# A six-layer local-attention kernel: weight splits and rotary products made once in the global stage, kept in DRAM, and fetched at the layer borders

## What is computed

```python
for i in range(DEPTH):                                   # DEPTH = 6
    x = attn_layer(shift_tokens(x), Wqkv[i], q_scale[i], k_scale[i], Wo[i]) + x
    x = ffn_layer(shift_tokens(x), ln_g[i], ln_b[i], W1[i], b1[i], W2[i], b2[i]) + x
# attn_layer: 16 heads of 64, q and k normalised, scaled by q_scale/k_scale, turned by rotary
# tables that depend on the position, attention inside windows of 32 tokens and the one before
```

## Time and profile before

| what | us |
|---|---|
| median of 3 runs | 3338.78 (3337.55 to 3340.59) |
| the profiled execution | 3341.1 |
| its span, first to last instruction | 3339.3 |
| PE, DVE, ACT, POOL busy | 3236.8, 2646.8, 2627.2, 2300.2 |
| mean granted TensorE clock | 0.989 of full |

### The profile page before, as it was taken

How to read it: one execution, slowest core, us unless ns; L and a number is a source line. 1 busy time by engine, 2 the same in 40 slices (tenths; PEclk the granted TensorE clock), 3 DMA queues, 4 the chain that set the end, 5 groups by cost and what they waited for, 6 DMA issues and landing times. The chain is left out here.

```text
span 3339.3 us, 125688 instructions
## 1 busy us (share of the span) xinstructions
PE 3236.8 (97%) x50357; PEld 2579.0 (77%) x50357; DVE 2646.8 (79%) x6351; ACT 2627.2 (79%) x5453; POOL 2300.2 (69%) x1519
## 2 busy tenths in 40 slices
PE   7979999999999999999999999999999999999997
PEld 5758878877877877887877787877788777778785
DVE  4658878878888877887887888878788787888884
ACT  3448888888888888888888888888888888888883
POOL 2028777777777776777777777777777777777771
PEclk9989999999999999999999999999999999999998
DMA  2001111211211211211221111121111121111111
GB/s 88 3 4 50 44 41 48 69 39 41 56 44 40 73 42 40 55 45 40 56 58 42 49 49 42 40 72 43 47 48 45 40 73 40 49 43 49 42 40 48
DMA packets 98194, 156.51 MB, mean 47 GB/s; under 512 B 18128, under 2 KB 39632, under 8 KB 96720
## 3 DMA queue, kind: packets, MB, share of 16 engines
q1 hardware_dynamic: 93440, 132.73, 14.8%
q10 hardware_dynamic: 4176, 15.74, 1.4%
HBM read 20.48 MB, written 2.10 MB: 7 GB/s over the span
## 5 line engine op out<-in xcount | busy, mean ns | idle before, releaser
L316 POOL TENSOR_TENSOR qks<-work 128x1024 f32<-128x1024 f32 x384 | 910.5, 2371 | 113.3 <-issue 105.7
L324 POOL TENSOR_TENSOR qkr<-qks,rnorm 128x1024 f32<-128x1024 f32 x384 | 731.4, 1905 | 307.6 <-issue 221.5
L493 ACT ACTIVATE sq<-psum 128x512 f32<-128x512 f32 x768 | 461.4, 601 | 234.8 <-PE psum L737 233.2
L332 POOL TENSOR_TENSOR probn<-prob,psumr 128x512 f32<-128x512 f32 x384 | 400.5, 1043 | 303.3 <-DVE psumr L1104 303.3
L737 PE MATMUL psum<-whi,xhi 128*128 128x512 f32 x1152 | 552.5, 480 | 24.6 <-POOL xlo L341 18.6
L1056 DVE TENSOR_REDUCE ssq<-sq 128x8 f32<-128x512 f32 x768 | 519.9, 677 | 8.1 <-ACT sq L493 7.9
L1080 DVE TENSOR_TENSOR work<-psum,rot 128x512 f32<-128x512 f32 x768 | 508.8, 662 | 8.3 <-POOL qks L316 7.5
L757 PEld LDWEIGHTS psum<-kT,qbd 128*64 128x64 f32 x12288 | 392.3, 139 | 154.9 <-issue 100.4
L1098 DVE TENSOR_REDUCE psumr<-prob 128x8 f32<-128x512 f32 x384 | 261.9, 682 | 287.5 <-ACT prob L547 283.1
L737 PE MATMUL psum<-whi,xlo 128*128 128x512 f32 x1152 | 459.6, 399 | 0.0
L757 PE MATMUL psum<-kT,qbd 128*64 128x64 f32 x12288 | 445.6, 226 | 13.1 <-ACT kT L529 13.1
(11 more groups left out here) (131 smaller groups left out, 6385.7 us busy)
## 6 DMA issues: line engine op xcount, KB each, us to landing
vsh<-vtok SPq DMA_DIRECT2D x384, 192.0 KB, 2.5
vsh<-vtok SPq DMA_DIRECT2D x384, 64.0 KB, 2.7
xsh<-xs_in SPq DMA_DIRECT2D x192, 64.0 KB, 2.1
ff_x<-x_mid SPq DMA_DIRECT2D x96, 128.0 KB, 2.4
wqkv<-Wqkv_dram ACTq DMA_DIRECT2D x5, 1536.0 KB, 7.8
wo_next<-Wo_dram ACTq DMA_DIRECT2D x5, 512.0 KB, 10.6
xtok<-x_dram SPq DMA_DIRECT2D x4, 512.0 KB, 11.0
out_dram<-qkr SPq DMA_DIRECT2D x8, 256.0 KB, 2.6
```

The lines of the kernel that those rows point to most:

```text
L316: pool.tensor_tensor(qks[:, :, :], rcos, rsin, ALU.add).then_inc(s["add_ready"], 1)
L324: pool.tensor_tensor(qkr[:, n % 2, :, :], qks[:, :, :], rnorm[:, :].unsqueeze(2).to_broadcast([P, 2 * OCT, DH]), ALU.mult).then_inc(s["qkr ...
L332: pool.tensor_tensor(probn[:, :, :], prob[:, n % 2, :, :], psumr[:, n % 2, 1, :].unsqueeze(2).to_broadcast([P, OCT, KEYS]), ALU.mult).then ...
L493: act.activation(sq[:, w * OCT:(w + 1) * OCT, :], bank[w].rearrange("p (h n) -> p h n", n=DH), ACT.Square).then_inc(s[("sqq_ready", "sqk_r ...
```

## The change

The splits of all six layers and the products of rotary table and scales of all six layers are made by POOL in the global stage, and those of layers 1 to 5 are written to DRAM by SP. POOL first makes six rotary products of 128x2048 (`rotary_gains(layer)`), then 18 pieces of weights (`weights_split(j)`, three a layer, each a copy of 128x1024 for the high part and a subtraction of 128x1024 for the low part). `global_inverse(1)` to `global_inverse(5)` stand between the groups of three pieces; numbers 6 and 7 stand behind all of it and behind three memsets. SP fetches the raw pieces of 512 KB (two in flight), and stores five rotary products and 15 pieces of 1 MB each; two staging buffers each, so that POOL waits for the store before last.

In the loop SP fetches a section (512 KB, high and low part) into its place as soon as PE has made the last projection of the old layer with it: the sections of q and k of the even units at step -2 of the border, those of the odd units at step -1, those of v at steps 1 and 2. It fetches the rotary products of a half sequence (512 KB) at steps -6 and 2, and `wo` straight into its place at step 6, all in its one queue behind `values_shifted` of the same step and ahead of `x_half` of the next. ACT's and POOL's split instructions, the copy of `wo`, POOL's `rotary_gains` and the two DMAs of ACT's queue are gone from the loop. Several buffers of the loop (`kT`, `qbd`, `vtok` among them) lie over the staging buffers; their memsets come behind the last store, and PE's first projection waits for them (`overlays_set`). The weights lie in DRAM in the order of the sections, which the host arranges.

```diff
@@ constants and buffers
+SECTION_AT = {wo: k for k, wo in enumerate(SECTIONS)}
+PIECES = len(SECTIONS) // 2
...
-        rot = sb("rot", [P, TPI, 2, 2, DH])
-        wqkv = sb("wqkv", [P, 3, INNER])
-        whi = sb("whi", [P, 3, INNER], F32R)
-        wlo = sb("wlo", [P, 3, INNER], F32R)
+        rot = sb("rot", [P, TPB, 2, 2, DH])
+        wparts = sb("wparts", [P, len(SECTIONS), 2, 512], F32R)
-        wo_next = sb("wo_next", [P, INNER // P, D])
...
+        with ExitStack() as early:
+            rot_raw = early.enter_context(nc.sbuf_tensor("rot_raw", [P, TPB, 2 * 2 * DH], F32))
+            qk_gain = early.enter_context(nc.sbuf_tensor("qk_gain", [P, DEPTH, 2 * 2 * DH], F32))
+            wraw = early.enter_context(nc.sbuf_tensor("wraw", [P, 2, 2, 512], F32))
+            rstage = shared("rstage", [P, 2, TPB, 2 * 2 * DH])
+            wstage = early.enter_context(nc.sbuf_tensor("wstage", [P, 2, 2, 2, 512], F32R))
...
+        wsplit = nc.dram_tensor("wsplit", (DEPTH - 1, len(SECTIONS), P, 2 * 512), F32, kind="Internal").ap()
+        rsplit = nc.dram_tensor("rsplit", (DEPTH - 1, P, TPB * 2 * 2 * DH), F32, kind="Internal").ap()
@@ sync
-            sp.dma_start(wqkv[:, :, :].rearrange("p k n -> p (k n)"), Wqkv[0]).then_inc(s["wqkv_in"], 16)
+            def raw_fetched(j):
+                layer, k = j // PIECES, j % PIECES
+                sp.dma_start(wraw[:, j % 2, :, :].rearrange("p s n -> p (s n)"), Wqkv[layer][:, k * 1024:(k + 1) * 1024]).then_inc(wraw_in[j % 2], 16)
+
+            def split_stored(j):
+                layer, k = j // PIECES, j % PIECES
+                sp.dma_start(wsplit[layer - 1, 2 * k:2 * k + 2].rearrange("s p n -> p s n"),
+                             wstage[:, j % 2, :, :, :].bitcast(F32).rearrange("p s h n -> p s (h n)")).then_inc(w_stored[j % 2], 16)
+
+            raw_fetched(0)
+            raw_fetched(1)
...
+            for layer in range(1, DEPTH):
+                sp.wait_ge(s["rot_made"], layer + 1)
+                sp.dma_start(rsplit[layer - 1], rstage[:, layer % 2, :, :].rearrange("p t n -> p (t n)")).then_inc(r_stored[layer % 2], 16)
+            for j in range(DEPTH * PIECES):
+                sp.wait_ge(s["w_lo"], j + 1)
+                if j + 2 < DEPTH * PIECES:
+                    raw_fetched(j + 2)
+                if j >= PIECES:
+                    split_stored(j)
+
+            def section_renewed(layer, k):
+                if layer is None:
+                    return
+                w, oc = SECTIONS[k]
+                if layer == 1 and k == 0:
+                    for half in range(2):
+                        sp.wait_ge(w_stored[half], 16 * ((DEPTH * PIECES - PIECES + half) // 2))
+                sp.wait_ge(s[("projq_ready", "projk_ready", "vp_ready")[w]], layer * UNITS - 1 + oc)
+                sp.dma_start(wparts[:, k, :, :].bitcast(F32).rearrange("p h n -> p (h n)"), wsplit[layer - 1, k]).then_inc(wparts_in[k], 16)
+
+            def rotation_renewed(layer, half):
...
+                sp.wait_ge(s["rotk_ready"], layer * UNITS - (1 - half) * UNROLL)
+                sp.dma_start(rot[:, half * TPI:(half + 1) * TPI, :, :, :].rearrange("p t k n d -> p (t k n d)"),
+                             rsplit[layer - 1][:, half * TPI * 4 * DH:(half + 1) * TPI * 4 * DH]).then_inc(rot_in[half], 16)
+
+            def output_renewed(layer):
...
+                sp.wait_ge(s["wo_ready"], layer * TILES)
+                sp.dma_start(wo[:, :, :].rearrange("p k n -> p (k n)"), Wo[layer]).then_inc(s["wo_in"], 16)
@@ sync, the loop over steps
                 x_half(step)
                 ffn_fetched(block_at(step, 1))
                 values_shifted(step - 4)
+                rotation_renewed(renewed_at(step, -6), 0)
+                section_renewed(renewed_at(step, -2), SECTION_AT[0, 0])
+                section_renewed(renewed_at(step, -2), SECTION_AT[1, 0])
+                section_renewed(renewed_at(step, -1), SECTION_AT[0, 1])
+                section_renewed(renewed_at(step, -1), SECTION_AT[1, 1])
+                section_renewed(renewed_at(step, 1), SECTION_AT[2, 0])
+                section_renewed(renewed_at(step, 2), SECTION_AT[2, 1])
+                rotation_renewed(renewed_at(step, 2), 1)
+                output_renewed(renewed_at(step, 6))
@@ gpsimd
+            def rotary_gains(layer):
+                if layer >= 3:
+                    pool.wait_ge(r_stored[layer % 2], 16 * ((layer - 1) // 2))
+                dst = rstage[:, layer % 2, :, :] if layer else rot[:, :, :, :, :].rearrange("p t k n d -> p t (k n d)")
+                pool.tensor_tensor(dst, rot_raw[:, :, :], qk_gain[:, layer:layer + 1, :].to_broadcast([P, TPB, 4 * DH]),
+                                   ALU.mult).then_inc(s["rot_made"], 1)
+
+            def weights_split(j):
+                layer, k, slot = j // PIECES, j % PIECES, j % 2
+                pool.wait_ge(wraw_in[slot], 16 * (j // 2 + 1))
+                if j in (PIECES, PIECES + 1):
+                    pool.wait_ge(r_stored[1], 16 * 3)
+                    pool.wait_ge(r_stored[0], 16 * 2)
+                elif layer:
+                    pool.wait_ge(w_stored[slot], 16 * ((j - PIECES) // 2))
+                parts = wstage[:, slot, :, :, :] if layer else wparts[:, 2 * k:2 * k + 2, :, :]
+                pool.tensor_copy(parts[:, :, 0, :], wraw[:, slot, :, :]).then_inc(s["w_hi"], 1)
+                pool.wait_ge(s["w_hi"], j + 1)
+                pool.tensor_tensor(parts[:, :, 1, :], wraw[:, slot, :, :], parts[:, :, 0, :].bitcast(F32), ALU.subtract).then_inc(s["w_lo"], 1)
 
             global_inverse(0)
-            for k in range(len(SECTIONS)):
-                weights_low(0, k)
-            for n in range(1, 2 * B):
+            pool.wait_ge(s["gain_in"], 16 * 2)
+            for layer in range(DEPTH):
+                rotary_gains(layer)
+            for j in range(DEPTH * PIECES):
+                if j and j % PIECES == 0:
+                    global_inverse(j // PIECES)
+                weights_split(j)
+            for half in range(2):
+                pool.wait_ge(w_stored[half], 16 * ((DEPTH * PIECES - PIECES + half) // 2))
+            pool.memset(kT[:, :, 0:WIN], 0.0)
+            pool.memset(qbd[:, :, :, :, :], 0.0)
+            pool.memset(vtok[:, 1, :, :], 0.0).then_inc(s["overlays_set"], 1)
+            for n in range(DEPTH, 2 * B):
                 global_inverse(n)
...
-                low_renewed(renewed_at(step, -1), 0, 1)
-                low_renewed(renewed_at(step, 0), 2, 3)
-                low_renewed(renewed_at(step, 2), 4)
-                low_renewed(renewed_at(step, 3), 5)
-                rotary_gains(step)
                 x_low(step)
@@ scalar
-                    if i in (1, 2, 3) and b == 0:
-                        weights_high(0, 2 * i - 2)
-                        weights_high(0, 2 * i - 1)
...
-                weights_fetched(renewed_at(step, -8))
-                output_renewed(renewed_at(step, 6))
-                high_renewed(renewed_at(step, -1), 0, 1)
-                high_renewed(renewed_at(step, 0), 2, 3)
-                high_renewed(renewed_at(step, 2), 4)
-                high_renewed(renewed_at(step, 3), 5)
@@ tensor, project
-                if n % UNITS < UPT:
-                    pe.wait_ge(s["w_lo"], n // UNITS * len(SECTIONS) + ((0, 1), (2, 3), (4, 5))[oc if w < 2 else 2][w if w < 2 else oc] + 1)
+                if n % UNITS < UPT and n >= UNITS:
+                    pe.wait_ge(wparts_in[SECTION_AT[w, oc]], n // UNITS * 16)
@@ vector, rotation
-                need(dve, "rot_made", n // UPT + 1)
+                if w == 0 and n == 0:
+                    dve.wait_ge(s["rot_made"], 1)
+                if w == 0 and layer and n % UNITS in (0, UNROLL):
+                    dve.wait_ge(rot_in[ti // TPI], layer * 16)
```

More of the change, by code:

```diff
@@ L76, in sb, with shared @@
             return ctx.enter_context(nc.sbuf_tensor(name, shape, dt))
+        def shared(name, shape):
+            with nc.sbuf_tensor(name, shape, F32) as t:
+                return t
         def sem(name):
@@ L185, in build @@
         vsh_in = [sem(f"vsh_in{k}") for k in range(2 * UPT)]
+        wraw_in = [sem(f"wraw_in{k}") for k in range(2)]
+        w_stored = [sem(f"w_stored{k}") for k in range(2)]
+        r_stored = [sem(f"r_stored{k}") for k in range(2)]
+        wparts_in = [sem(f"wparts_in{k}") for k in range(len(SECTIONS))]
+        rot_in = [sem(f"rot_in{k}") for k in range(2)]
         block = ctx.enter_context(nc.Block())
@@ L204, in _ @@
             sp.dma_start(w2[:, :, :].rearrange("p k n -> p (k n)"), W2[0]).then_inc(s["w2_in"], 16)
+            for layer in range(1, DEPTH):
[17 more added lines that the diff above has]
+            def rotation_renewed(layer, half):
+                if layer is None:
+                    return
+                if layer == 1 and half == 0:
+                    sp.wait_ge(r_stored[1], 16 * 3)
+                    sp.wait_ge(r_stored[0], 16 * 2)
```

(48 more changed lines are left out.)

34 lines of the change are left out of this document (14 added, 20 removed).

## The result

The changed kernel took **3359.6 us** (median of 4 runs, 3351.8 to 3366.3), the kernel before 3339.2 beside it: a ratio of 1.0060 with a 95% interval of 1.0041 to 1.0079. It is slower by 20 us, the side that was forecast; the forecast of 3348.5 was 11 low, inside its range. A second set of runs of the same kernel gave 3358.1 (3353.0 to 3360.9), ratio 1.0056 (1.0043 to 1.0070).

A forecast was written before the change was run, and what follows sets the result against it. PE, busy for 97% of the span, was taken as the bound. For the profiled execution 3341.1 + 16 + 2 + 18 + 1 - 27.0 - 0.4 = 3350.7 us, so a median of 3348.5; range 3317 to 3366.

The forecast's parts named there:

- The bound and the border before: Loop: PE busy throughout steady steps, eight taking 62.94 us; each layer border costs 7.5 us extra, five of them 37.5.
- What the border keeps: Layer borders: 2.1 us of the 7.5 stay at each, so five save 27.0 (low end 15, high end 34).
- The stall of 1.2: Border: PE's wait for `xlo`, whose fetch SP issues behind its wait for the k projection; 1.2 us taken.
- The high end: Border: x lands at 710.8 behind the sections in the queue, and PE stalls 2.6 us, as today.
- Rival 3: Borders: x fetch comes late behind two sections, 4 to 4.5 us stay each, 16 saved; 3359.5 us, chance 0.12.
- The contention: Global stage: DVE waits for POOL's instructions through their shared port; 16 + 2 + 18 us, and 1 for lower clock.
- the 0.4 of the last norm: Head of the loop: the POOL product at 220.40 no longer holds up the global stage's last norm; 0.4 us gained.
- The clamp: Start of global stage: DVE's four instructions clamping the gates each wait behind a POOL product; 16 us taken.
- the values: Global stage: DVE's two two-input instructions for sequence 0 run beside POOL's last products; 0 to 5 us, taken 2.
- the norms: Global stage, norms 1 to 5: POOL gets between DVE's eight instructions; 5 us each odd, 1.5 each even, 18.
- rival 1: Global stage: DVE keeps the port in its runs, so contention and clock cost 19 us; 3330.5 us, chance 0.28.
- POOL's prices: Global stage: POOL takes 4.7 us a product, 2.5 a subtraction, 1.2 a copy; 95 us in all.

The follow-up runs named there:

- x first: Changed kernel with the fetch of x for a layer's first step issued ahead of the two section fetches of the step before; 3340.8 us.
- x between: Changed kernel with the fetch of x for a layer's first step issued between the two section fetches of the step before; 3342.2 us.

## Why the prediction was right, point by point

**The bound and the border before: right.** Steady steps stayed at 62.94, and the five borders cost 36.3 against the 37.5 worked out from the first one.

**What the border keeps: the mechanism right, the size wrong.** This is the term that was mis-sized. The forecast had 27.0 saved, 2.1 us left at a border; the trace has 18.4 saved, 3.6 left, and four other traces 12 to 15 saved. The places of the issues were right: 1.4 and 1.9 us after the k projection begins (1.5 and 2.1 worked out). What failed was the landing. The stall of 1.2 supposes 3.0 us from the second issue of x to ACT's start, 0.9 over the 2.1 of a lone x; at the five borders it was 3.3 to 4.9. So PE stalled for 1.4 to 3.0, 2.3 in the mean, and the lower clock followed at three of the five: 3.4 us each at half the rate, by estimate 1.0 a border where 0.4 was taken. The high end (2.6, "as today") was the near one, and it was itself added up too low: 2.8 on top of the 708.5 is 711.3, not 710.8, a stall of 3.1. Rival 3, the late x, is what happened at the borders, and its time, 3359.5, is the measured median; it was given 0.12, too little for a term whose low and high ends lay 2.3 us apart five times over.

**The contention: right, and the working nearly so.** Forecast 16 + 2 + 18 + 1 = 37 us in the global stage, less the 0.4 of the last norm, measured 33.5. The clamp took 15.9 longer (16 taken) and ended 14.6 later, since it began 1.3 earlier when its inputs landed earlier; the values took 2.4 longer (2 taken), the norms 16.9 (18 taken), and the last norm gained the 0.4. 14.6 + 2.4 + 16.9 - 0.4 is the whole 33.5, so nothing is left for the lower clock, taken at 1. POOL and DVE took turns, as in the forecast and not as in rival 1, and the two-input instructions waited as the others did. By the Trainium skill, *SBUF — State Buffer*, section "Who interferes with whom", both kinds of DVE instruction contend with a POOL instruction that reads; the trace agrees, with 3.66 and 4.60 us for the clamp's `tensor_scalar` (0.43 alone) and 4.98 and 4.87 for its two-input ones (0.68 alone). DVE's slack, for which 1 us was taken off each odd norm, hid nothing.

**POOL's prices: right.** 4.50 us a product alone, 4.75 with its waits for DVE (4.7 taken), 1.04 a copy (1.2), 2.36 a subtraction (2.5); in all 90 us (95). **The rest: right.** No inverse came late, `wo` and the sections were covered, the stores (6.4 us to landing) made POOL pause once in each gap, which even ended the turn-taking early.

In sum, for the profiled execution: 3.1 too dear in the global stage (36.6 against 33.5), 8.6 too much saved at the borders, and 4.3 too little at the two ends of the loop, for which the forecast had nothing. These cancel: 3350.7 - 3.1 + 8.6 - 4.3 is 3351.9, and 3351.8 was measured. That the profiled execution comes out 1 us from the sum is luck. The median shows the miss: the forecast took the profiled execution as 2.3 above it, and after the change it lies 7.8 below, since the borders of that one execution were cheap.

## What to carry to other kernels

Work that is moved to an idle engine can be paid for by the engine that shares a port with it: list that engine's SBUF-to-SBUF instructions in the stage, and hold the moved work back until each group of them is done. Here three kinds of wait and a new order turned 34 us of loss into none, with POOL's work unchanged. And a wait put into an in-order queue of DMAs is paid by what stands behind it: put the small transfer that is wanted next ahead of the wait, and don't price its landing behind large ones as if it were alone (here 3.3 to 4.9 us instead of 2.1).

## What the runs showed that I had not expected

- POOL and DVE take turns strictly where both read, one instruction each; beside fills a DVE `tensor_scalar` waited for three in a row, 4.39 us where it needs 0.43.
- From the fastest run to the slowest the changed kernel spreads over 14.5 us, the kernel before over 3 (and 4 to 7 in the larger sets); with x first the borders are gone and the spread is still 10 (3335.4 to 3345.3). Here too the slower runs have the lower mean granted clock: 0.989 in the fastest, 0.985 or 0.986 in the five above 3344. The traces of x first and x between, which differ in the borders alone, put some of it at the ends of the loop: the first eight steps took 45.8 and 49.7 us, what follows the last row of `xlo` 114.7 and 112.1. What decides it is open.
